# The first tile's last two probability transpositions behind the second tile's scores on TensorE

## The chip, the cores and the metric

One NeuronCore of a Trainium2 chip runs the whole program. The metric is device time in microseconds, the median of several runs. Lower is better.

## The reference

A cross-attention layer and a mixture-of-experts layer, each behind a layer norm and with a residual. The input x is 4 x 1024 x 256, the context 4 x 77 x 256, all in float32.

```python
x = x + xattn(layernorm(x), ctx, ctx, mask, Wq, bq, Wk, bk, Wv, bv, Wo, bo)   # 16 heads of 16, 77 keys
x = x + ffn(layernorm(x), gate_weight, bias, experts_gate_up, experts_down, shared_gate, shared_up, shared_down)
# xattn: softmax(q k^T / 4 where mask, else -1e9) v, then Wo and bo
# ffn:   sigmoid gate over 32 experts, the best 4 of 8 groups, then the best 6 experts, weights scaled to 2.5
#        out = sum over the 6 of w_e * (silu(x Wg_e) * (x Wu_e)) Wd_e  +  one shared expert of width 256
```

## The kernel before

The 4096 token rows are 32 tiles of 128 rows (NT = 32; t is a tile's number). The first part of the program carries each tile through attention, the second layer norm, the gate, the ranking of tokens by expert and the scattering of rows to an HBM table sorted by expert. A middle part turns counts into block addresses. The last part runs 224 blocks of 128 rows through their experts, in 112 pairs, and adds each token's six results.

Each engine has its program written out in order by `over_tiles(step)`: for n from -1 to 37, `step` lists stages, and `at_tile(tile, lag, stage)` issues the stage for tile t = n - lag if there is one. So the order of the `at_tile` lines is the order on the engine. A stage begins with waits on semaphores (`need`, `freed`, `read_out`, `wait_ge`), and what is listed behind a waiting stage waits as well.

The stages that matter here, for n = 0 and n = 1:

- TensorE: `qk` (L766 four mask products in bf16, L770 eight score products in fp32) writes the scores of tile n to `sc_ps`. It needs `qT` of its tile, and that VectorE has read the scores of the tile before (`score_sub`). `tr_x` (L740) transposes the normed x of tile n+1, `q_proj` (L750) projects it. `v_chunks` (L728), at n = 0 only, spreads the value rows over ten chunks of 128. `tr_p(f)` (L792) transposes the probabilities of a tile: 1232 columns are ten chunks (NCH = 10), `tr_p(0)` and `tr_p(1)` take four each and run at lag 1, `tr_p(2)` takes the last two and runs at lag 0, as the last stage of a step. `pv(0..2)` (L804) multiplies them with the values. `tr_o` (L815), `o_proj` (L825, L826) follow at lag 2.
- VectorE: `row_max` (L1136) and `shift` (L1144), two halves each, read the scores and write the unnormalised logits to `probs`. At n = 1 between them and the next tile's stand `late_values` (L1098: ten products that move the value chunks from PSUM to SBUF, each adding one to `vbd_ready`), then for later n `late_bias` (L1061 to L1069), `late_stats` (L1028) and the stages of older tiles (`inverse_sums` L1154, `normalise` L1159, `residual` L1166).
- ScalarE: `exps` (L591, the exponential), `ev_q` (L585, copies q with its bias to `qT`), `norm1` (L573), `ev_pT(2)` (L600), `ev_xT` (L579), `ev_pT(0)` (L600), in this order within a step. `ev_pT(1)` of a tile is first in the next step.
- GpSimd: `inverse_std` (L513) and the scattering (L493 fill, L503 indirect DMA), six rows of it for a tile.

`tr_p(2)` begins with these lines, so for the first tile it waits for the exponential and for all ten products of `late_values`. Its PSUM bank held value chunks 6 and 7.

```python
need(pe, "probs", t)
if t == 0:
    need(pe, "probs_zero", 0)
    pe.wait_ge(S_["vbd_ready"], B + NCH)
```

Of the kernel before, what the change touches and what calls it, by code (L numbers as in the profile page):

```python
# [99 lines left out]
def build(nc, x, mask, wq, wk, wv, wo, bqk, bvo, ctx_t, gate_w, gate_b, egu, edn, sgu, sdn, const_in, ids_in, out):  # L100
# [7 lines left out]
    with ExitStack() as ctx:  # L108
# [189 lines left out]
        def need(eng, name, t, per=1):  # L298
            eng.wait_ge(S_[name], (t + 1) * per)
# [10 lines left out]
        def read_out(eng, name, t, ahead):  # L310

            n = t + ahead + 1
            if not isinstance(n, int):
                eng.wait_ge(S_[name], n)
            elif n > 0:
                eng.wait_ge(S_[name], min(n, NT))
# [10 lines left out]
        def over_tiles(step):  # L327
            for n in range(-LEAD, NT + LAG):
                def tile(lag, n=n):
                    t = n - lag  # L330
                    return (t, t % UA, t // B) if 0 <= t < NT else None
                step(tile)

        def at_tile(tile, lag, stage):
            got = tile(lag)
            if got is not None:
                stage(*got)
# [9 lines left out]
        def load_table(engine, row, j, n, top):  # L347
            _, got = nc.values_load_multi_w_load_instructions(
                table[0:1, row * P + j:row * P + j + n], engines=(engine,), min_val=0, max_val=top,
                skip_runtime_bounds_check_because="the table's entries are clipped to this range where it is made")  # L350
            return got
# [338 lines left out]
        def _(pe):  # L690
# [27 lines left out]
            def v_chunks(c0, c1):  # L718
                def stage(t, m, s):
                    if t:  # L720
                        return
                    if c0 == 0:
                        need(pe, "vrows", 0, 2)
                    for c in range(c0, c1):
                        off, n0 = c * P % C, chunk_head(c) * DH
                        if c >= 6:
                            pe.wait_ge(S_["vbd_ready"], B + c // 2 * 2 - 4)
                        mm(vchunk[c].rearrange("p (b n) -> p b n", b=B), const("rep")[0:C, off:off + P],  # L728
                           vrows[0:C, :, n0:n0 + 3 * DH], start=True, stop=True).then_inc(S_["vchunk_ps"], 1)
                return stage  # L730
# [44 lines left out]
            def tr_p(f):  # L775
                def stage(t, m, s):
                    if f == 0:
                        read_out(pe, "o", t, -1)
                    if f == 1:
                        read_out(pe, "gate_exp", t, -3)  # L780
                        if 1 <= t <= 2:
                            read_out(pe, "pT1", t, -1)
                    if f == 2:
# [4 lines that stand above are left out]
                        read_out(pe, "x1", t, -2)  # L788
                        if 1 <= t <= 1:
                            read_out(pe, "pT2", t, -1)  # L790
                    for c in range(4 * f, min(4 * f + 4, NCH)):
                        last = nc.tensor.transpose(pT_ps[f][:, (c % 4) * P:(c % 4 + 1) * P],  # L792
                                                   probs[:, m % 2, c * P:(c + 1) * P], ident)
                    last.then_inc(S_[f"pT_ps{f}"], 1)
                return stage

            def pv(f):
                def stage(t, m, s):
                    need(pe, f"pT{f}", t)
                    if f == 0:  # L800
                        read_out(pe, "pT0", t, 0)
                    for c in range(4 * f, min(4 * f + 4, NCH)):
                        n0 = chunk_head(c) * PV
                        last = mm(pv_ps[:, n0:n0 + 3 * PV], pT[:, c, :], vbd[:, m, c, :, :].rearrange("p a b -> p (a b)"),  # L804
                                  start=c == 0, stop=c == NCH - 1, skip_group_check=True)
                    last.then_inc(S_["pv"], 1)
                return stage
# [71 lines left out]
            def s_up(s, h, gs=(0, 1)):  # L879
                xs = store[:, s * B * D:(s + 1) * B * D].rearrange("p (b k n) -> p k b n", b=B, k=KT)  # L880
                if s > SE:
                    pe.wait_ge(S_["shh"], 4 * (s - SE - 1) + 2 * h + 2)
                for g in gs:
                    for k in range(KT):
                        last = mm(ps8[2 * h + g].rearrange("p (b n) -> p b n", b=B),  # L885
                                  wsgu[:, k, g * SI + h * P:g * SI + (h + 1) * P],
                                  xs[:, k, :, :], start=k == 0, stop=k == KT - 1)
                if 1 in gs:
                    last.then_inc(S_["sg_ps"], 1)
# [14 lines left out]
            def count_chosen(t0, t1):  # L904
                for t in range(t0, t1):
                    last = mm(cum_ps, sel[:, t, :], stepb[:, NT - t:2 * NT + 1 - t], start=t == 0, stop=t == NT - 1)
                if t1 == NT:
                    last.then_inc(S_["cum_ps"], 1)

            def s_early(t, m, s):  # L910
                if t == NT - 3:
                    pe.wait_ge(S_["score_sub"], NT)
                if t >= NT - 3:
                    i = t - (NT - 3)
                    s_up(SE, i // 2, (i % 2,))

            def count_early(t, m, s):
                if t == NT - 1:
                    s_up(SE, 1, (1,))
                    count_chosen(0, NT - 2)  # L920

            def step(tile):
                at_tile(tile, 4, gate)
                at_tile(tile, 0, qk)
                at_tile(tile, -1, tr_x)
                at_tile(tile, -1, v_last)
                at_tile(tile, 0, v_chunks(0, 6))
                at_tile(tile, 2, tr_o)
                at_tile(tile, 1, tr_p(0))
                at_tile(tile, 1, tr_p(1))  # L930
                at_tile(tile, -1, q_proj)
                at_tile(tile, 2, o_proj)
                at_tile(tile, 3, tr_x2)
                at_tile(tile, 0, v_chunks(6, NCH))
                at_tile(tile, 4, up)
                at_tile(tile, 5, dn)
                at_tile(tile, 3, s_early)
                at_tile(tile, 4, count_early)
                at_tile(tile, 1, pv(0))
                at_tile(tile, 1, pv(1))  # L940
                at_tile(tile, 1, pv(2))
                at_tile(tile, 4, rank)
                at_tile(tile, 0, tr_p(2))
            over_tiles(step)


# [596 lines left out]
```

## Time and profile before

| | before |
|---|---|
| runs | 802.43, 800.10, 798.34 us; median 800.1 |
| the profiled execution | 801.02 us, its span 799.2 us (1.8 us lie around it) |
| TensorE busy | 734.8 us, 92% |
| VectorE / ScalarE / GpSimd busy | 522.0 (65%) / 389.7 (49%) / 535.6 us (67%) |
| mean granted TensorE clock | 0.959 |

The times of instructions are from one profiled execution and count from the start of its span. A granted clock of 1.00 is 2.4 GHz and 0.50 is 1.2 GHz. The trace counts some fp32 matmuls twice (eight score products are x16, four value products x8), transpositions once.

### The profile page before, as it was taken

How to read it: one execution, taken by the hardware profiler on the slowest of the kernel's cores; microseconds unless marked ns; L12 is line 12 of the kernel's file. 1: busy time of each engine (PE TensorE's matmuls, PEld its weight loads, DVE VectorE, ACT ScalarE, POOL GpSimd, SP SyncE). 2: the span in 40 equal slices, each digit the busy share in tenths (PEclk: the TensorE clock that was granted, in tenths of full speed). 3: DMA queues.
4: the chain of work that ended last, by engine and by line, in shares of the span. 5: the costliest groups of instructions: out<-in, count | busy, mean ns of one | idle time of the engine just before them, and what ended most of it. 6: DMA issues, size and time to landing. Idle time of an engine off the chain costs nothing.

```text
span 799.2 us, 18242 instructions
## 1 busy us (share of the span) xinstructions
PE 734.8 (92%) x5768; PEld 652.1 (82%) x5768; DVE 522.0 (65%) x1628; ACT 389.7 (49%) x832; POOL 535.6 (67%) x788
## 2 busy tenths in 40 slices
PE   6899999999999999986859999999999999999980
PEld 3789888888888888873449999998988999888970
DVE  4897777778777777665444425676775766566663
ACT  2455445444454445431026666666565666555550
POOL 0115788878787888877700007888888788987885
PEclk9899999999999999887879999999999999999995
DMA  9213443333344423432345557798888888878863
GB/s 272 94 54 100 126 133 120 120 115 131 119 133 126 134 100 126 138 120 100 107 159 170 173 167 231 243 279 248 262 261 257 252 263 250 257 239 253 259 214 108
DMA packets 97295, 140.13 MB, mean 175 GB/s; under 512 B 14944, under 2 KB 69732, under 8 KB 97201
## 3 DMA queue, kind: packets, MB, share of 16 engines
q1 hardware_dynamic: 77112, 87.50, 34.7%
q0 software_dynamic: 18432, 50.36, 20.3%
q10 hardware_dynamic: 1656, 1.10, 0.5%
q8 instruction: 48, 0.79, 0.5%
q14 instruction: 47, 0.38, 0.2%
HBM read 75.98 MB, written 62.94 MB: 174 GB/s over the span
## 4 chain that ended last, share of the span: by engine, by line
PE 36%; POOL 32%; issue 14%; DVE 8%; another core or an unknown queue 4%; DMA 2%; ACT 1%; DVEq 1%; POOLq 0%; ACTq 0%; SPq 0%
POOL rows L503 19%; PE sc_ps L994 19%; PE bank L1006 10%; POOL work L493 8%; PE sc_ps L978 4%; POOL work L541 2%; POOL rstd L513 2%; DVE firsts L1028 1%; DMA store<-in_x 1%; PE bank L898 1%; DMA work<-yrows,dest 1%; DVE work L1144 1%; DVE mx L1136 1%; PE sc_ps L885 1%
## 5 line engine op out<-in xcount | busy, mean ns | idle before, releaser
L994 PE MATMUL sc_ps<-work 128*128 128x128 f32 x1792 | 221.2, 277 | 5.9 <-DVE work L1491 2.9
L994 PEld LDWEIGHTS sc_ps<-work 128*128 128x128 f32 x1792 | 210.3, 193 | 8.7 <-issue 5.0
L541 POOL DMA_INDIRECT work<-yrows,dest x192 | 188.3, 981 | 35.6 <-POOL work L493 22.6
L503 POOL DMA_INDIRECT rows<-work,dest x192 | 187.7, 977 | 34.9 <-issue 34.8
L493 POOL MEMSET work<- 128x304 f32 (+1 forms) x360 | 136.6, 379 | 95.0 <-DMA yrows<-work 86.3
L1006 PE MATMUL bank<-wdn,work 128*128 x448 | 116.6, 383 | 5.3 <-DVE work L1446 3.3
L1446 DVE TENSOR_TENSOR work<-work,sc_ps 128x256 f32<-128x256 f32 x112 | 47.0, 419 | 113.3 <-ACT work L659 65.7
L1472 DVE SCALAR_TENSOR_TENSOR work<-work 128x256 f32<-128x256 f32 x160 | 76.9, 481 | 19.1 <-DMA work<-yrows,dest 12.7
L680 ACT ACTIVATE work<-bank 128x512 f32<-128x512 f32 x112 | 66.9, 597 | 45.5 <-PE bank L1006 25.7
L1006 PEld LDWEIGHTS bank<-wdn,work 128*128 128x128 f32 x448 | 76.5, 191 | 13.4 <-issue 7.6
L591 ACT ACTIVATE work<-work 128x1232 f32<-128x1232 f32 x32 | 39.4, 1231 | 91.1 <-DVE work L1144 81.7
L654 ACT ACTIVATE work<-sc_ps 128x512 f32<-128x512 f32 x112 | 66.7, 595 | 33.8 <-PE sc_ps L978 24.0
L659 ACT ACTIVATE work<-sc_ps 128x256 f32<-128x256 f32 x112 | 42.8, 383 | 75.2 <-PE sc_ps L994 34.1
L804 PEld LDWEIGHTS bank<-work 128*128 128x128 f32 x640 | 76.0, 192 | 1.8 <-issue 0.5
L672 ACT ACTIVATE work<-wgu 128x512 f32 x112 | 70.7, 632 | 8.8 <-issue 8.8
L804 PE MATMUL bank<-work 128*128 128x51 f32 x640 | 74.7, 272 | 0.0
L978 PE MATMUL sc_ps<-cst,work 128*128 128x128 f32 x448 | 67.7, 274 | 0.8 <-issue 0.8
L600 ACT ACTIVATE work<-bank 128x512 f32<-128x512 f32 (+1 forms) x96 | 47.3, 525 | 39.0 <-PE bank L792 38.4
L978 PEld LDWEIGHTS sc_ps<-cst,work 128*128 128x128 f32 x448 | 56.2, 142 | 12.4 <-issue 1.5
L513 POOL TENSOR_TENSOR rstd<-var,cst 128x1 f32<-128x1 f32 x32 | 18.1, 565 | 71.4 <-DVE var L1180 71.0
L1491 DVE COPY work<-wgu 128x512 f32 x112 | 57.4, 513 | 12.9 <-issue 11.3
L1136 DVE TENSOR_REDUCE mx<-sc_ps 128x8 f32<-128x616 f32 x64 | 50.8, 794 | 4.0 <-PE sc_ps L770 4.0
(173 smaller groups left out, 1108.5 us busy)
## 6 DMA issues: line engine op xcount, KB each, us to landing
work<-rows SPq DMA_DIRECT2D x224, 128.0 KB
yrows<-work SPq DMA_DIRECT2D x112, 256.0 KB
wgu<-in_egu SPq DMA_DIRECT2D x16, 512.0 KB
store<-in_x SPq DMA_DIRECT2D x8, 512.0 KB, 12.0
wdn<-in_edn SPq DMA_DIRECT2D x8, 512.0 KB
rows<-padrow SPq DMA_DIRECT2D x8, 512.0 KB
out<-work SPq DMA_DIRECT2D x32, 128.0 KB
rows<-work,dest POOLq DMA_INDIRECT x192
```

The lines of the kernel that those rows point to most:

```text
L493: pool.memset(dead, 0.0).then_inc(S_["gap"], 1)
L503: pool.indirect_dma_start(rows[:, :], bass.IndirectOffsetOnAxis(ap=dest[:, t, k:k + 1], axis=0), rowb[:, m, :], None).then_inc(scat[m], 16)
L541: pool.indirect_dma_start(yg[:, g % RG, :], None, yrows[0:2 * n * P, :], bass.IndirectOffsetOnAxis(ap=dest[:, t, k:k + 1], axis=0)).then_i ...
L654: a.activation(xeT[:, m % 2, :], ps8[m % 2], ACT.Copy).then_inc(S_["xeT"], 1)
L672: a.activation(wst[1][m % 2], wgu[:, bass.ds(named.pop(2 * i + 1) * 512, 512)], ACT.Copy).then_inc(S_["laid1"], 1)
L680: a.activation(ye[:, i % YP, :], ps8[6 + m % 2], ACT.Copy).then_inc(S_["ye"], 1)
L804: last = mm(pv_ps[:, n0:n0 + 3 * PV], pT[:, c, :], vbd[:, m, c, :, :].rearrange("p a b -> p (a b)"), start=c == 0, stop=c == NCH - 1, skip ...
L978: last = nc.tensor.transpose(ps8[m % 2][:, (2 * w + k) * P:(2 * w + k + 1) * P], xe[:, j % RX, k * P:(k + 1) * P], ident)
L994: last = mm(ps8[2 + m % 2][:, (2 * w + g) * P:(2 * w + g + 1) * P], wst[w][m % 2][:, k * 2 * I + g * I:k * 2 * I + (g + 1) * I], xeT[:, m ...
L1006: last = mm(ps8[6 + m % 2][:, w * D:(w + 1) * D], hid[:, m % 2, w * P:(w + 1) * P], wdn[:, bass.ds(e * D, D)], start=True, stop=True)
L1136: red(mx4[:, 2 * half:2 * half + 2, :], four(half), AX.X, ALU.max).then_inc(S_[f"score_max{half}"], 1)
L1472: v.scalar_tensor_tensor(outb[:, t % 3, :], yg[:, g % RG, :], slotw[:, t % 2, k:k + 1], so_far, ALU.mult, ALU.add).then_inc(S_["part"], 1)
```

## The change

The last two transpositions of tile 0's probabilities, `tr_p(2)` for t = 0, are issued in step n = 1, ahead of `tr_p(0)`, and no longer at the end of step n = 0. For every other tile `tr_p(2)` stays where it was. No wait is taken away or added, and no instruction.

```diff
+            def first_tr_p(t, m, s):
+                if t == 0:
+                    tr_p(2)(t, m, s)
+
+            def later_tr_p(t, m, s):
+                if t:
+                    tr_p(2)(t, m, s)
+
...
                 at_tile(tile, 2, tr_o)
+                at_tile(tile, 1, first_tr_p)
                 at_tile(tile, 1, tr_p(0))
                 at_tile(tile, 1, tr_p(1))
...
                 at_tile(tile, 1, pv(2))
                 at_tile(tile, 4, rank)
-                at_tile(tile, 0, tr_p(2))
+                at_tile(tile, 0, later_tr_p)
```

The only place where TensorE's order differs is the passage from step n = 0 to step n = 1. Before, its rows read (L728 value chunks, L792 the two transpositions, L766 and L770 tile 1's scores, L740 tile 2's x, L792 the other eight of tile 0, L750 tile 2's q):

```order
L750 MATMUL bank<-work 128x128 x3
L728 MATMUL bank<-wdn,cst 128x192 [waits vbd_ready] x4
L792 MATMUL bank<-cst,work 128x128 [waits vbd_ready,probs_zero,probs]
L792 MATMUL bank<-cst,work 128x128
L766 MATMUL sc_ps<-work 128x308 [waits score_sub,qT]
L766 MATMUL sc_ps<-work 128x308 x3
L770 MATMUL sc_ps<-work 128x154 x8
L740 MATMUL bank<-cst,work 128x128 [waits qT,xn]
L740 MATMUL bank<-cst,work 128x128
L792 MATMUL bank<-cst,work 128x128 x8
L750 MATMUL bank<-work 128x128 [waits xnT]
```

In the changed kernel the same place on TensorE reads:

```order
L750 MATMUL bank<-work 128x128 x3
L728 MATMUL bank<-wdn,cst 128x192 [waits vbd_ready] x4
L766 MATMUL sc_ps<-work 128x308 [waits score_sub,qT]
L766 MATMUL sc_ps<-work 128x308 x3
L770 MATMUL sc_ps<-work 128x154 x8
L740 MATMUL bank<-cst,work 128x128 [waits qT,xn]
L740 MATMUL bank<-cst,work 128x128
L792 MATMUL bank<-cst,work 128x128 [waits vbd_ready,probs_zero,probs]
L792 MATMUL bank<-cst,work 128x128 x9
L750 MATMUL bank<-work 128x128 [waits xnT]
```

The two transpositions, with their wait for the ten value products and the exponential, moved behind twelve score products and two transpositions of x. They now stand in one row with the other eight.

## Rows read from the trace of the kernel before

**Rows 1.** The page: the span, and TensorE's busy time, share and instructions.

```profile
span 799.2 us, 18242 instructions
PE 734.8 (92%) x5768; PEld 652.1 (82%) x5768; DVE 522.0 (65%) x1628; ACT 389.7 (49%) x832; POOL 535.6 (67%) x788
```

**Rows 2.** Windows, middle of the tile loop: stretch, length, busy by engine, PEclk, DMA share, GB/s.

```profile
100.00:150.00 50.00, 49.88 (x447) 44.83 (x446) 38.20 (x144) 23.45 (x55) 40.89 (x63) 1.00 0.41 130
...
200.00:250.00 50.00, 49.66 (x457) 44.48 (x456) 36.91 (x137) 24.38 (x60) 39.16 (x62) 1.00 0.39 125
```

**Rows 3.** The chain that ended last, 24 to 30 us: start, length, what.

```profile
24.64 1.58 PE bank L728 x8
...
27.02 0.66 PE bank L792 x2
27.68 1.03 PE sc_ps L766 x4
28.70 1.39 PE sc_ps L770 x16
```

**Rows 4.** Timeline, 23 to 31 us: start, length, instruction [idle before <- releaser].

```profile
23.26 0.80 DVE L1144 TENSOR_TENSOR work<-sc_ps,mx 128x616 f32<-128x616 f32 x1
23.98 2.90 DVE L1098 TENSOR_TENSOR work<-bank,cst 128x192 f32<-128x192 f32 x10
24.09 1.23 ACT L591 ACTIVATE work<-work 128x1232 f32<-128x1232 f32 x1 [2.64 <-DVE work L1144]
...
25.23 0.61 ACT L585 ACTIVATE work<-bank,bias_qk 128x128 f32<-128x128 f32 x2
...
27.02 0.66 PE L792 MATMUL bank<-cst,work 128*128 128x128 f32 x2 [0.81 <-DVE work L1098]
...
27.71 0.38 ACT L600 ACTIVATE work<-bank 128x256 f32<-128x256 f32 x1 [1.39 <-PE bank L792]
...
30.11 0.80 DVE L1136 TENSOR_REDUCE mx<-sc_ps 128x8 f32<-128x616 f32 x1 [3.17 <-PE sc_ps L770]
...
30.70 0.38 ACT L579 ACTIVATE work<-bank 128x256 f32<-128x256 f32 x1 [2.60 <-PE bank L740]
```

**Rows 5.** Windows around the changed place, columns as in group 2.

```profile
24.00:26.00 2.00, 1.36 (x8) 1.27 (x8) 2.00 (x9) 1.91 (x4) 0.00 (x0) 1.00 0.60 208
26.00:28.00 2.00, 1.19 (x7) 0.73 (x6) 0.92 (x4) 0.61 (x2) 0.00 (x0) 0.74 0.09 21
28.00:30.00 2.00, 2.00 (x20) 1.20 (x18) 0.00 (x0) 0.10 (x1) 0.00 (x0) 0.50 0.00 0
...
32.00:34.00 2.00, 2.00 (x13) 2.00 (x11) 1.90 (x5) 1.43 (x3) 0.00 (x0) 0.56 0.00 0
```

**Rows 6.** Timeline, TensorE: tile 2's scores, 36 to 38 us.

```profile
36.23 0.69 PE L766 MATMUL sc_ps<-work 77*128 77x308 bf16 x4
...
36.85 0.81 PE L770 MATMUL sc_ps<-work 32*128 32x154 f32 x16
```

**Rows 7.** Timeline, VectorE and TensorE, 36 to 39 us.

```profile
36.86 1.40 DVE L1028 BATCH_NORM_STATS2 firsts<-store 128x6 f32<-128x256 f32 x4
...
38.18 0.24 DVE L1154 RECIPROCAL rsum<-bank 128x16 f32<-128x16 f32 x1
...
38.79 0.79 DVE L1136 TENSOR_REDUCE mx<-sc_ps 128x8 f32<-128x616 f32 x1
38.93 0.20 PEld L815 LDWEIGHTS bank<-cst,work 128*128 128x128 f32 x2 [1.14 <-DVE work L1159]
```

**Rows 8.** Windows where the clock falls the second time, columns as in group 2.

```profile
50.00:55.00 5.00, 4.56 (x41) 4.04 (x44) 4.58 (x20) 3.07 (x7) 0.52 (x1) 0.93 0.14 22
55.00:60.00 5.00, 5.00 (x41) 4.27 (x33) 4.47 (x14) 1.85 (x4) 2.91 (x2) 0.73 0.24 84
```

**Rows 9.** Windows in the end of the tile loop and the middle part, as in group 2.

```profile
325.00:330.00 5.00, 3.60 (x26) 3.01 (x25) 3.10 (x14) 3.08 (x7) 4.49 (x7) 0.73 0.55 185
...
360.00:365.00 5.00, 5.00 (x14) 2.27 (x13) 1.55 (x8) 0.38 (x1) 2.31 (x4) 0.51 0.53 184
```

## The prediction

> **What bounds the kernel now.** I read the page first: TensorE is busy 92% of 799.2 us [rows 1]. The windows then say where: in the middle of the tile loop it is busy 49.88 and 49.66 of 50 us [rows 2]. There every tile waits for TensorE, and a tile loop that begins earlier ends earlier. Nothing in that stretch is touched by the change. What it touches is one place near 27 us, ahead of this full stretch, so I asked the chain of waits and the timeline for that place.
>
> The chain runs there through the value products (L728, to 24.64 + 1.58 = 26.22), a hole, the two transpositions at 27.02 and then tile 1's scores, 27.68 to 28.70 + 1.39 = 30.09 [rows 3]. The timeline names the hole: TensorE stood idle 0.81 us before L792, released by VectorE's L1098, the ten value products that end at 23.98 + 2.90 = 26.88. VectorE itself then stood 3.17 us idle until the scores came, at 30.11 [rows 4]. So at this place the engine that is waited for is TensorE, and TensorE waits for something that the scores do not need.
>
> **What the change does here.** What do the scores of tile 1 need? That VectorE has read tile 0's (L1144 ends at 23.26 + 0.80 = 24.06) and their q (L585 ends at 25.23 + 0.61 = 25.84) [rows 4]. Both are there before TensorE is through with L728 at 26.22. In the changed kernel the scores can start right behind it, at about 26.25.
>
> How long do they take? At the full clock the same twelve products took from 36.23 to 36.85 + 0.81 = 37.66, that is 1.43 us [rows 6]. In this place they took 2.41 us, since the clock was low: the granted clock is 1.00 in 24 to 26, 0.74 in 26 to 28, and 0.50 in 28 to 30 [rows 5]. From the 0.74 the fall lies near 26 + 2 x 0.48 = 26.96 us, if it is one step from 1.00 to 0.50.
>
> - No fall: scores ready at 26.25 + 1.43 = 27.68. Against 30.09 that is 2.4 us.
> - Fall at the same moment, 26.96: 0.71 us of the work is done, the other 0.72 us goes at the low clock. The low clock takes 1.39 us for L770 [rows 3] where the full one takes 0.81 [rows 6], 1.7 times as long: 1.23 us. Scores ready at 28.2, a gain of 1.9 us.
> - Low clock all through: 26.25 + 2.42 = 28.67, a gain of 1.4 us.
>
> I take 1.9, the middle one and the one that keeps the clock of the trace. Of it 0.8 us is the idle time taken away, 0.66 us the two transpositions that no longer stand ahead, and the rest is the score work that gets ahead of the fall.
>
> The two transpositions themselves cost the same as before, 0.66 us at the low clock, and are paid behind the scores. Who waits for them? On ScalarE `ev_pT(2)` (L600 at 27.71) now waits for them, and behind it in ScalarE's order stand `ev_xT` (L579, 30.70) and `ev_pT(0)`. Tile 2's x is transposed behind the scores, two transpositions like the 0.66 us at 27.02 [rows 3], so by 28.9; the two moved ones are done by 29.6, L600 (0.38 us) by 30.0 and L579 by 30.4. Before, it began at 30.70 after an idle time of 2.60 us [rows 4]. So the new order on ScalarE costs nothing; a transposition that was waiting for an idle engine still meets an idle engine. Its cover is TensorE's own eight transpositions that stand ahead of `q_proj`. Of the values L1098 is done at 26.88, well before 28.9, so the moved wait is empty. SP's and GpSimd's queues are not passed by anything.
>
> **Does the gain live until 60 us?** From 30.11 to 38.79 VectorE works almost without a gap: tile 1's maxima and shifts, the bias pieces, statistics (36.86 to 38.26), the reciprocal at 38.18, then tile 2's row maximum at 38.79. Tile 2's scores were ready at 37.66, 1.1 us before VectorE took them, and TensorE stood idle 1.14 us (weight loads) at 38.93 for VectorE's L1159 [rows 6, 7]. So VectorE sets the pace and all of it moves up by 1.9 us, provided that TensorE keeps up. TensorE's work from here to 37.66 is one piece without idle time, starts 0.77 us earlier (26.25 for 27.02) and so ends at about 36.9. VectorE would ask at 38.79 - 1.9 = 36.9. That just holds. With no fall of the clock, TensorE has far more room. After that, the next stages hang on one another by semaphores, not on an outside time: DMA is at a share of 0.00 from 28 us on [rows 5], so the loads that the start needed have landed. Once TensorE is full, it is full 1.9 us earlier.
>
> **Sum.** 801.0 - 1.9 = 799.1 us for an execution like the profiled one, and 800.1 - 1.9 = 798.2 us against the median, 0.9 us below that execution. It is 0.24%, and the three runs of before spread over 4.1 us. A measurement of this kernel can tell about 0.5%, 4 us; so the verdict should be no change.
>
> **The clock as a rule.** The clock fell after a stretch in which TensorE was busy 1.36 of 2 and 1.19 of 2 us [rows 5]. The change fills 0.8 us of that. The Trainium skill, TensorE: Matmul & The Clock Gate, Part 1, says that the gate follows how busy the array has been, and that the monitor runs freely and is not reset when a kernel starts, so that the place of a transition varies from run to run. By this rule the fall at 27 us may not come at all, and falls elsewhere may shift; the sum would then be 800.1 - 2.4 = 797.7 us by the first bullet's number. The trace agrees in that the clock fell behind idle time; one trace can't show whether the place varies.
>
> **Rivals.**
>
> 1. *The forecast*: 1.4 to 2.4 us come out at the end, 797.7 to 798.7 us. For it: the chain goes through this very place, and the engine behind it is idle 3.17 us. Against it: several steps of the tile loop lie between 38 us and the full stretch, and I followed only the first of them number by number. Chance 0.62.
> 2. *Swallowed*: the gain is used up before TensorE is full, by a later wait that I read as moving along. For it: TensorE still waits for others at 38.93 [rows 7], and the margin above (36.9 against 36.9) is nil. It would give 800.1 us, with 799.5 to 800.7 about it. Chance 0.14.
> 3. *A second fall is saved too*: in 50 to 60 us the granted clock is 0.93 and 0.73, which is 5 x 0.07 + 5 x 0.27 = 1.7 us of work lost while TensorE was busy 4.56 and 5.00 of 5 us [rows 8]. If the earlier start changes what TensorE does before it so that this fall stays away, the time is 800.1 - 2.4 - 1.7 = 796.0 us. Nothing in the change aims at it. Chance 0.10.
> 4. *Slower: a fall where TensorE is full*. A faster TensorE at 27 to 37 us waits longer for VectorE at 38.9 (1.14 us now, up to about 2 us then), and idle time is what the clock fell behind at 27. If the clock then falls for as long as from 27 to 34 us (0.52 + 1.0 + 1.0 + 0.88 = 3.4 us of work, taking 30 to 32 us as 28 to 30 [rows 5]), TensorE has about 1 us of slack a tile to pay it with and owes 2.4. If one more such fall comes in the end part, where the clock is already 0.73 and 0.51 in places with TensorE busy [rows 9], 3.4 us more are owed. The first alone gives 800.1 - 2.4 + 2.4 = 800.1 us; it decides for slower from the point where the lost work is over 3.4 us, and with 3.4 more it is 803.5 us. Chance of a time over 800.7: 0.14.
>
> **How the numbers follow.** The range takes the forecast's own width (797.7 to 798.7), the swallowed case above it, half of the way to rival 3 and the nearer part of rival 4. It has to hold the scatter of a median too, which in the runs shown is up to 2 us either way. 796.0 to 801.3 us leaves out about 0.18. Faster by over 0.5% (under 796.1 us) needs rival 3 or a lucky median: 0.08. Slower by over 0.5% (over 804.1 us) needs rival 4 with a second fall: 0.03. The same: 0.89.
>
> **What would show it.** In the profile after: L766 right behind L728 near 26.3 us, without the 0.81 us idle time; the row maximum at 27.7 to 28.7 us for 30.11; L792 as one group of ten behind L740; ScalarE's L579 no later than 30.7; the row maximum of tile 2 near 36.9 us for 38.79; GpSimd's first scatter about 1.9 us earlier. I am wrong if the scores start late because q or L1144 isn't there, if VectorE's stages at 38 us don't move by as much as those at 30, or if the first scatter moves and the end doesn't, which would be the clock in the end part.

## The result, and the profile after

| | before | changed |
|---|---|---|
| median of 22 runs each, side by side | 798.46 us (789.64 to 807.26) | 793.80 us (786.10 to 803.46) |
| ratio changed / before | | 0.9952, 95% interval 0.9930 to 0.9975 |
| the profiled execution | 801.02 us, span 799.2 | 793.72 us, span 791.9 |
| mean granted clock of it | 0.959 | 0.968 |

The ratio is worked out from the fast runs alone, those within 1.5% of the fastest of their kernel, so it is not the quotient of the two medians, 0.9942. The changed kernel is faster by 0.48%, just inside the 0.5% that I had called no change, and beyond its interval. I had said 798.2 us, from 796.0 to 801.3; 793.8 lies outside. Of the 4.4 us by which I missed, 1.6 us is the base: the kernel before has a median of 798.46 us in 22 runs, not 800.1 as in three. By the ratio, the gain is 798.46 x 0.0048 = 3.8 us (2.0 to 5.6 by its interval), where I had 1.9.

The chain of waits of the changed kernel, 24 to 29 us (start, length, what), answers to [rows 3]:

```profile
24.65 1.57 PE bank L728 x8
26.22 0.52 PE sc_ps L766 x4
26.74 0.78 PE sc_ps L770 x16
27.55 0.81 DVE mx L1145
```

The hole is gone: the scores follow the value products at once. The lines of VectorE are nine further down than before, so L1145 is the row maximum. The timeline of the changed kernel for the same place answers to [rows 4, 7]; its columns are start, length, instruction, and in brackets the idle time before it and what ended it:

```profile
23.98 2.90 DVE L1107 TENSOR_TENSOR work<-bank,cst 128x192 f32<-128x192 f32 x10
...
26.06 0.69 PE L766 MATMUL sc_ps<-work 77*128 77x308 bf16 x4
...
26.67 0.81 PE L770 MATMUL sc_ps<-work 32*128 32x154 f32 x16
...
27.55 0.80 DVE L1145 TENSOR_REDUCE mx<-sc_ps 128x8 f32<-128x616 f32 x1 [0.59 <-PE sc_ps L770]
...
27.68 1.26 PE L792 MATMUL bank<-cst,work 128*128 128x128 f32 x10
28.10 0.39 ACT L600 ACTIVATE work<-bank 128x256 f32<-128x256 f32 x1 [1.77 <-PE bank L792]
...
28.38 0.38 ACT L579 ACTIVATE work<-bank 128x256 f32<-128x256 f32 x1
...
36.22 0.79 DVE L1145 TENSOR_REDUCE mx<-sc_ps 128x8 f32<-128x616 f32 x1
36.35 0.20 PEld L815 LDWEIGHTS bank<-cst,work 128*128 128x128 f32 x2 [2.24 <-DVE work L1168]
```

The scores ran at the full clock, 0.69 and 0.81 us, where they had taken 1.03 and 1.39. The row maximum comes at 27.55 for 30.11, tile 2's at 36.22 for 38.79: 2.56 and 2.57 us. ScalarE's L579 comes 2.3 us earlier, so the moved pair holds up nobody there. TensorE now waits 2.24 us for VectorE at 36.35, for 1.14 before.

What becomes of the 2.57 us? GpSimd's L513 runs once a tile, so its starts are good milestones for the tile loop. For tiles 0, 1 and 2 the changed kernel has

```profile
44.76 0.55 POOL L513 TENSOR_TENSOR rstd<-var,cst 128x1 f32<-128x1 f32 x1 [21.44 <-DVE var L1189]
52.91 0.55 POOL L513 TENSOR_TENSOR rstd<-var,cst 128x1 f32<-128x1 f32 x1 [7.60 <-DVE var L1189]
...
62.63 0.54 POOL L513 TENSOR_TENSOR rstd<-var,cst 128x1 f32<-128x1 f32 x1 [6.29 <-DVE var L1189]
```

and the kernel before

```profile
46.33 0.55 POOL L513 TENSOR_TENSOR rstd<-var,cst 128x1 f32<-128x1 f32 x1 [23.03 <-DVE var L1180]
54.48 0.55 POOL L513 TENSOR_TENSOR rstd<-var,cst 128x1 f32<-128x1 f32 x1 [7.60 <-DVE var L1180]
...
65.76 0.54 POOL L513 TENSOR_TENSOR rstd<-var,cst 128x1 f32<-128x1 f32 x1 [7.85 <-DVE var L1180]
```

So 1.57 us is left at tile 0, and 3.13 us at tile 2. Both steps come where the clock differs. The windows of the changed kernel (stretch, length, busy time of TensorE, its weight loads, VectorE, ScalarE and GpSimd, then the granted clock, the DMA share and GB/s):

```profile
24.00:34.00 10.00, 9.27 (x91) 7.83 (x92) 9.04 (x25) 6.37 (x13) 0.00 (x0) 1.00 0.10 33
34.00:44.00 10.00, 8.00 (x50) 6.93 (x51) 8.78 (x23) 4.27 (x9) 0.00 (x0) 0.83 0.04 5
```

```profile
50.00:55.00 5.00, 4.57 (x49) 3.98 (x49) 4.50 (x21) 2.95 (x10) 2.09 (x2) 1.00 0.35 105
55.00:60.00 5.00, 5.00 (x42) 4.50 (x40) 3.96 (x14) 2.51 (x6) 1.34 (x1) 1.00 0.12 16
```

The fall at 27 us is gone, one at 37 us is new (0.83 in 34 to 44), and the fall at 54 us, 0.93 and 0.73 in [rows 8], is gone too. From tile 2 on the gain stays between 2.8 and 4.1 us to tile 29. The last 3.4 of the 7.3 us between the two spans come behind it, in the middle part and the expert part, where neither kernel's order was changed and the clock falls in both.

### The profile page after: what moved, and what is told of

Same layout as the page of the kernel before. It is cut to its first block, busy times and chain, and to the rows that moved or that the text cites. A ratio compares the mean times of both kernels' runs of the same rounds, so it can differ in the third digit from the quotient of the medians.

```text
span 791.9 us, 18242 instructions
## 1 busy us (share of the span) xinstructions
PE 727.0 (92%) x5768; PEld 647.6 (82%) x5768; DVE 521.1 (66%) x1628; ACT 389.0 (49%) x832; POOL 535.1 (68%) x788
## 4 chain that ended last, share of the span: by engine, by line
PE 37%; POOL 31%; issue 16%; DVE 6%; another core or an unknown queue 4%; DMA 3%; ACT 1%; SPq 1%; POOLq 0%; DVEq 0%; ACTq 0%
PE sc_ps L1003 20%; POOL rows L503 20%; PE bank L1015 10%; POOL work L493 7%; PE sc_ps L987 5%; POOL rstd L513 2%; DMA store<-in_x 2%; POOL work L541 2%; PE bank L898 1%; DMA yrows<-work 1%; PE bank L804 1%; ACT work L672 1%; DVE work L1153 1%; DVE mx L1145 0%
## 5 line engine op out<-in xcount | busy, mean ns | idle before, releaser
L804 PEld LDWEIGHTS bank<-work 128*128 128x128 f32 x640 | 75.9, 192 | 1.8 <-issue 0.5
L804 PE MATMUL bank<-work 128*128 128x51 f32 x640 | 74.7, 272 | 0.0
L513 POOL TENSOR_TENSOR rstd<-var,cst 128x1 f32<-128x1 f32 x32 | 18.1, 565 | 66.2 <-DVE var L1189 65.7
L1153 DVE TENSOR_TENSOR work<-sc_ps,mx 128x616 f32<-128x616 f32 x64 | 51.2, 799 | 1.2
```

Source lines behind the costliest of these rows:

```text
L1153: last = tt(probs[:, m % 2, 0:HC].rearrange("p (r h c) -> p r h c", r=4, h=4)[:, 2 * half:2 * half + 2], four(half), mx4[:, 2 * half:2 * h ...
```

## The experiments

Twelve runs, in three groups: c0, a1, e1, e2; then c1, e3, e4, e5; then c2, a2, e3b, e4b. The kernel before ran beside each group; its medians there were 780.9, 818.3 and 779.7 us. The first and the third group ran on one chip, the second on another, so chips differ by far more than the change is worth, and ratios are taken inside a group. In the profiles I count from the start of the last value products (L728 x8, 24.64 us in the first profile). In all profiles but a2 and e4 it lies between 23.57 and 24.65 us; in these two it comes at 30.04 and 29.33 us. In the table "max 1" is tile 1's row maximum, "rstd 0" to "rstd 20" are GpSimd's L513 of these tiles; "wait" is TensorE's idle time ahead of the first `tr_o`, where it waits for VectorE to normalise tile 0 (L1159 in the kernel before).

| profile | clock falls at, up to 130 us | max 1 | wait | rstd 0 | rstd 2 | rstd 20 |
|---|---|---|---|---|---|---|
| before, first | 27, 54 | 5.47 | 0.91 | 21.69 | 41.12 | 233.37 |
| c0, before | 27, 54 | 5.47 | 0.92 | 21.69 | 41.12 | 231.56 |
| c1, before (the slower chip) | 38 | 4.16 | 2.01 | 21.38 | 39.25 | 238.71 |
| c2, before | 27, 54 | 5.37 | 0.76 | 21.58 | 41.06 | 231.50 |
| changed, first | 37 | 2.90 | 2.00 | 20.11 | 37.98 | 229.36 |
| a1, changed | 35 | 2.89 | 2.01 | 21.31 | 39.17 | 229.62 |
| a2, changed | 15, 42 | 3.88 | 2.00 | 20.96 | 38.82 | 229.26 |
| e1, wait kept | 27 | 4.94 | 0.36 | 21.15 | 39.01 | 229.45 |
| e2, hole filled | 36 | 4.12 | 2.01 | 21.13 | 38.98 | 229.42 |
| e3, stats late (the slower chip) | 104 | 2.90 | 0.70 | 17.16 | 34.42 | 235.99 |
| e3b, stats late | 123 | 2.89 | 0.70 | 17.15 | 34.41 | 227.74 |
| e4, second hole (the slower chip) | 15, 59 | 5.20 | none | 21.76 | 41.25 | 242.57 |
| e4b, second hole | 51 | 2.90 | 0.47 | 19.10 | 38.55 | 229.00 |
| e5, late hole (the slower chip) | 38 | 4.16 | 2.01 | 21.34 | 39.21 | 238.33 |

### Both kernels again: c0, a1, c1, a2, c2

No edit in any of them.

> The kernel before once more, unchanged, beside itself. What it tells: where the clock falls in another execution, and how far two medians of the same kernel lie apart. Theory A (the fall near 27 us belongs to the order of the work: TensorE idles 0.8 us there): the granted clock falls again between 24 and 30 us, tile 1's row maximum comes at 28.7 to 30.1 us, and the ratio is 1.000 within 0.4%. Theory B (the fall is chance, it came in the one profile that was read): no fall before 34 us, row maximum at about 28.9 us.

> The changed kernel once more. Theory A: no fall before 35 us, row maximum of tile 1 at 27.5 us as in its first profile, ratio 0.995. Theory B: the fall near 27 us can come here as well, the row maximum then at 28.2 us or later, and the ratio is 0.997 to 0.998, the 1.9 us of the forecast.

> The kernel before a third time, for the place of its falls alone. Theory A: falls near 27 and near 54 us again, tile 1's row maximum 5.5 us behind the value products, rstd of tile 1 to tile 2 in 11.3 us. Theory B: one of the falls is missing.

> The changed kernel a third time. Theory A (of the change's gain 1.1 to 1.3 us is order and shows at equal clock, the rest is clock time not lost, which varies from execution to execution): tile 1's row maximum 2.9 us behind the value products, a fall of the clock at 35 to 38 us, ratio 0.995 to 0.998; in a fit of the time by the clock time lost the kernel's own term is -1.1 us within its error. Theory B (the whole 3.8 us of the first comparison belong to the change, in every execution): ratio 0.995, own term -3 us or more.

> The kernel before a fourth time, for its falls before 60 us: near 27 and 54 us as in two executions, or at 38 us alone as in the third. The order part of the gain should be the difference of tile 1's row maximum between executions with no fall there, 4.16 - 2.90 = 1.26 us behind the value products; with a fall at 27 us it is 5.47 - 2.90 = 2.57 us.

Measured: before against itself 1.0014 (0.9979 to 1.0049); the changed kernel 0.9977 (0.9942 to 1.0011) and 0.9976 (0.9942 to 1.0009). Weighted by the widths of their intervals, the three comparisons of the changed kernel make 0.9963 +- 0.0016, that is 2.9 us +- 1.3.

Is the fall at 27 us the order's or chance's? Both have a part. Up to 52 us e5 has the order of before. So that order has five executions, and the fall came in three (the first profile, c0, c2), not in c1 and e5. It came in e1, which keeps the wait. It came in none of the five executions with the changed order that reached the place at the full clock (the first profile, a1, e3, e3b, e4b), nor in e2, where the wait is filled. That is four of six with the idle time and none of six without; a2 and e4, low from 15 us on, say nothing of it. Why the fall stayed away in c1 and e5 is not known. Timeline of c1, the kernel before with the full clock all through this place:

```profile
24.10 1.57 PE L728 MATMUL bank<-wdn,cst 77*128 77x192 f32 x8 [0.77 <-DVE work L1098]
...
26.48 0.41 PE L792 MATMUL bank<-cst,work 128*128 128x128 f32 x2 [0.81 <-DVE work L1098]
26.77 0.68 PE L766 MATMUL sc_ps<-work 77*128 77x308 bf16 x4
27.39 0.81 PE L770 MATMUL sc_ps<-work 32*128 32x154 f32 x16
...
28.26 0.80 DVE L1136 TENSOR_REDUCE mx<-sc_ps 128x8 f32<-128x616 f32 x1 [1.85 <-PE sc_ps L770]
```

The hole of 0.81 us stands there as in the others, and the row maximum comes 4.16 us behind the value products instead of 5.47. So the order alone is worth 4.16 - 2.90 = 1.26 us, and the fall at 27 adds 1.31 us in the executions that have it. e5 has the 4.16 as well, and the four other full-clock executions of the changed order 2.89 or 2.90. a2, the changed kernel, had a low clock from 15 to 32 us, which begins ahead of the change:

```profile
30.04 2.55 PE L728 MATMUL bank<-wdn,cst 77*128 77x192 f32 x8
...
33.92 0.80 DVE L1145 TENSOR_REDUCE mx<-sc_ps 128x8 f32<-128x616 f32 x1 [0.59 <-PE sc_ps L770]
...
42.73 0.69 PE L815 MATMUL bank<-cst,work 128*128 128x128 f32 x2 [2.00 <-DVE work L1168]
```

Its last value products begin 5.8 us later than in a1 (24.27), more than the change brings. Counted from there it is like the other two: 38.82 at tile 2 and 229.26 at tile 20.

The column "wait" shows a second pattern. In the six executions where TensorE waited 2.00 or 2.01 us for tile 0's output, the clock fell in that wait or up to 1.3 us behind it: three of the changed kernel (37, 35, 42 us), but also c1, e2 and e5 (38, 36, 38 us), which have the order of before. In the seven with a wait of 0.36 to 0.92 us it did not fall there. All six had tile 1's scores at the full clock, and the other executions at the full clock there (e3, e3b, e4b) have an edit that shortens this wait. So the longer wait comes with a full clock at 27 us, in either order, and the change alone does not open it. c1, with the order of before:

```profile
37.08 0.44 PE L815 MATMUL bank<-cst,work 128*128 128x128 f32 x2 [2.01 <-DVE work L1159]
```

How does a gain travel? On the faster chip a tile takes 10.58 us in the full stretch. From tile 2 to tile 20 it is 190.44 or 190.45 us in seven executions (c0, c2, a1, a2, e1, e2, e4b). a1 is 1.95 us ahead of c0 at tile 2 and 231.56 - 229.62 = 1.94 us ahead at tile 20, and 1.7 us at tile 31. In the span it is 0.3 us ahead, 777.1 for 777.4: the rest went behind the tile loop, where executions that were level differ by 2 to 3 us. The slower chip's tiles are less even, and so are those of the first comparison, where 3.13 us at tile 2 became 4.0 at tile 20.

But c1, the unchanged order with no fall at 27 us, is at 39.25 at tile 2 (e5 at 39.21; both on the slower chip), level with a1's 39.17. The 1.26 us of order that a1 had at tile 1 went in its longer low clock behind the 2.01 us wait. So how far the changed kernel is ahead depends on which falls the execution of before has: 1.9 to 3.1 us at tile 2 against one with falls at 27 and 54 us (41.06 to 41.12 for 37.98, 39.17 and 38.82), 0.1 to 1.3 us against c1.

The runs of the first and the third group come with their mean granted clock, so the time can be set against the clock time that each run lost, (1 - clock) x time, by a straight line with a term of its own for each kernel. In the first group there are 83 runs of five programs: 0.77 us for each us of clock lost, and 1.4 us of scatter left of about 4. The changed kernel's own term is -1.1 +- 0.5 us (one standard error) and in the third group -1.0 +- 0.5 (e3b -1.3, e4b -1.4); before against itself +0.2 +- 0.5. On the slower chip the line leaves 3.4 us of scatter and tells nothing. The mean clock lost is 31.1 us for before and 29.2 for a1 in the first group, 30.2 and 29.1 in the third. 1.9 x 0.77 = 1.5 us and 1.1 x 0.79 = 0.9 us would be the clock's part; but the two differences have standard errors of 1.7 and 1.4 us, so this part is not shown by the runs. The own term is the 1.26 us of the profiles within its error, as theory A said; B, -3 us in every execution, does not hold.

### e1: the wait kept

```diff
                 freed(pe, "score_sub", t, 1)
+                if t == 1:
+                    need(pe, "probs", 0)
+                    pe.wait_ge(S_["vbd_ready"], B + NCH)
```

> The changed order, but tile 1's scores still wait for the ten value products and the exponential, so the 0.8 us idle time stays and only the two transpositions are out of the way. Theory A: the clock falls near 27 us as before, row maximum of tile 1 at 27.0 + 2.4 = 29.4 us, that is 0.7 us of gain; ratio 0.999. Theory B (the gain at this place is order alone): 28.5 us at the full clock or 29.4 us at the low one, as chance has it.

Measured: 0.9982 (0.9939 to 1.0024), own term -0.8 +- 0.5 us. In its timeline TensorE waits and the low clock is back:

```profile
24.18 1.57 PE L728 MATMUL bank<-wdn,cst 77*128 77x192 f32 x8 [0.77 <-DVE work L1110]
26.55 1.16 PE L769 MATMUL sc_ps<-work 77*128 77x308 bf16 x4 [0.81 <-DVE work L1110]
27.64 1.41 PE L773 MATMUL sc_ps<-work 32*128 32x154 f32 x16
```

Row maximum 4.94 us behind the value products; 29.4 - 24.6 = 4.8 was expected from the fall and the two transpositions out of the way. A gain of only 0.53 us there. Yet at tile 2 it is 2.11 us ahead of the kernel before, as far as a1, and stays there, since the fall at 54 us did not come. So that much at tile 2 can be had with the wait kept. It is one execution, and theory B's low-clock case, 29.4 us, is the same number: e1 alone does not tell A from B.

### e2: the hole filled

```diff
                            vrows[0:C, :, n0:n0 + 3 * DH], start=True, stop=True).then_inc(S_["vchunk_ps"], 1)
+                    if c1 == NCH:
+                        for _ in range(6 if c == NCH - 1 else 0):
+                            nc.tensor.transpose(sc_ps[:, 3, 320:320 + P], ident, ident)
```

> The order of before, with six transpositions of the identity matrix put into the idle time, into unused columns of the scores' PSUM; their results are read by nobody. The dependencies stay as before. Theory A: TensorE no longer idles at 26.2 to 27.0 us, the clock does not fall there, and tile 1's row maximum comes at 27.0 + 0.4 + 1.4 = 28.9 us instead of 30.1, so that half of the change's gain comes with nothing moved; ratio 0.997 to 0.998. Theory B (the clock is chance and the fill does nothing): row maximum at 30.1 us where the clock falls, ratio 1.000 or a little above.

Measured: 0.9944 (0.9907 to 0.9980); I had expected 0.997 to 0.998. The medians, 778.29 us beside 780.93, give 0.9966. Timeline, with the filling as L732:

```profile
23.57 1.57 PE L728 MATMUL bank<-wdn,cst 77*128 77x192 f32 x8 [0.77 <-DVE work L1101]
...
24.98 0.82 PE L732 MATMUL sc_ps<-cst 128*128 128x128 f32 x6
...
25.95 0.41 PE L795 MATMUL bank<-cst,work 128*128 128x128 f32 x2
...
27.69 0.80 DVE L1139 TENSOR_REDUCE mx<-sc_ps 128x8 f32<-128x616 f32 x1 [1.81 <-PE sc_ps L773]
```

Row maximum 4.12 us behind, 4.26 expected: with nothing moved and TensorE kept at work, the scores come 1.35 us earlier. One profile does not show that the filling did it, since c1 and e5 have 4.16 with the wait left empty. The runs support it: the 12 of e2 lie between 775.9 and 779.1 us, narrower than any other set of nine runs or more, and lost 26.9 us of clock on the mean for 31.1, a difference of 4.2 us with a standard error of 1.0. Its own term is -0.7 +- 0.5 us, though in this place the filled kernel does the same work in the same order; I take it as a measure of how far such a term can be trusted: the -1.1 and -1.0 of the changed kernel are not much further from nothing than this.

### e4: the second hole filled

TensorE's new wait at 36 us, in the changed kernel. The wait of `tr_o` for ScalarE's copy of `pT2` stands ahead of the filling.

```diff
             def tr_o(t, m, s):
-                need(pe, "o", t)
                 read_out(pe, "pT2", t, 1)
+                if t == 0:
+                    for _ in range(14):
+                        nc.tensor.transpose(bank[0][:, 320:320 + P], ident, ident)
+                need(pe, "o", t)
```

> The changed kernel with 14 transpositions of the identity matrix in the 2.0 us in which TensorE waits for tile 0's normalised output at 34.4 to 36.4 us; nobody reads them. Theory A (the earlier start opens a longer wait at 36 us, behind which the clock falls and takes back 1.0 us in one profile and 2.2 us in the other): no fall between 30 and 45 us, the first GpSimd rstd comes 2.6 us before that of the kernel before, counted from the value products at 24.6 us, that is 19.1 us behind them for 20.1 and 21.3; ratio 0.993 to 0.996. Theory B (the fall at 36 us is chance): it comes or stays away as it likes, no earlier rstd than 20.1.

> The changed kernel with 14 idle transpositions in the 2 us wait at 34.4 to 36.4 us, a second time, since the first profile had a long low clock from 15 us on, ahead of its edit. Theory A (the fall at 35 to 38 us hangs on this idle time): with a full clock at the start, no fall at 35 to 38 us and the first rstd 19.1 us behind the value products for 20.1 and 21.3 in the changed kernel. Theory B (it does not): a fall there as in the changed kernel, 20.1 us or more.

The first profile had the low clock from 15 to 39 us, ahead of the edit, and the four runs give 1.0143 (1.0078 to 1.0208). Why they are slower is open: the one profile has its low clock ahead of the filling, and the twelve runs of e4b on the faster chip are not slower. The second: 0.9953 (0.9919 to 0.9988). Its windows, and its timeline around the filling (L813):

```profile
24.00:34.00 10.00, 9.71 (x95) 8.28 (x96) 8.89 (x24) 6.09 (x14) 0.00 (x0) 1.00 0.09 28
34.00:44.00 10.00, 9.06 (x82) 7.73 (x80) 9.13 (x25) 4.42 (x9) 0.55 (x1) 1.00 0.08 17
...
50.00:60.00 10.00, 9.91 (x78) 8.80 (x78) 7.53 (x26) 5.16 (x12) 3.43 (x2) 0.83 0.31 77
```

```profile
33.74 1.69 PE L813 MATMUL bank<-cst 128*128 128x128 f32 x14
35.91 0.44 PE L818 MATMUL bank<-cst,work 128*128 128x128 f32 x2 [0.47 <-DVE work L1171]
```

No fall at 35 to 38 us, and the first rstd 19.10 us behind the value products, the 19.1 expected, for 20.11 and 21.31. All 2.6 us of the early gain are there at tile 0. Then the clock fell at 51 us, and tile 2 was reached at 38.55. So the fall at 36 us is what eats the early gain in the changed kernel. This is one execution, but it fits the column "wait": all six executions with the 2 us wait fell there, and the filled one did not. When one fall is removed another may come.

### e3: the statistics later

```diff
-                if t == 1:
-                    x_stats(4)
-                if t == 2:
-                    x_stats(5)
-                    x_stats(6)
-                if t == 3:
-                    x_stats(7)
+                if 5 <= t <= 8:
+                    x_stats(t - 1)
+                if t == 8:
                     x_variance(2)
-                if t == 9:
+                if t == 11:
                     x_shift(2)
...
-                if t == 1:
+                if t == 6:
                     inverse_part(2)
```

> The changed kernel, with VectorE's statistics of tiles 16 to 31 (28 us of starting tiles before, 5.6 us of VectorE work between 34 and 52 us) taken in steps 6 to 9 instead of 2 to 4, where TensorE sets the pace. Theory A (the stretch from 27 to 60 us is VectorE's, and a microsecond gained there lives to the end of the tile loop): TensorE no longer waits 2 us at 36 us, tile 2's GpSimd rstd comes 3 us or more before the changed kernel's, ratio to before 0.990 to 0.993. Theory B (gains ahead of the full stretch are swallowed): the rstd of tile 10 comes at the changed kernel's time, ratio 0.995 to 0.998.

> The changed kernel with the statistics of tiles 16 to 31 taken later, a second time, beside the changed kernel itself. Theory A (what is gained before TensorE is full lives on): the rstd of tile 2 about 34.4 us behind the value products for 38 to 39, and that of tile 20 at least 3 us before the changed kernel's in the same call; ratio 0.990 to 0.994. Theory B (the later statistics take back what they gave, VectorE holding up TensorE in steps 6 to 9): tile 20 no earlier than the changed kernel's, ratio 0.995 to 0.999.

Measured: 0.9991 (0.9936 to 1.0045) and 0.9980 (0.9937 to 1.0023). The early part did what it should: no wait at 36 us, tile 2 at 34.4 us behind the value products, 6.6 us ahead of the kernel before in the same group for e3b (c2) and 4.8 us for e3 (c1). Then it is lost again. GpSimd's rows of e3b, 100 to 136 us:

```profile
100.92 0.57 POOL L513 TENSOR_TENSOR rstd<-var,cst 128x1 f32<-128x1 f32 x1 [1.15 <-DVE var L1185]
101.47 2.91 POOL L477 TENSOR_TENSOR rstd<-firsts,cst 128x16 f32<-128x16 f32 x1
113.34 0.58 POOL L513 TENSOR_TENSOR rstd<-var,cst 128x1 f32<-128x1 f32 x1
123.25 0.57 POOL L513 TENSOR_TENSOR rstd<-var,cst 128x1 f32<-128x1 f32 x1 [0.40 <-DVE var L1185]
135.38 0.57 POOL L513 TENSOR_TENSOR rstd<-var,cst 128x1 f32<-128x1 f32 x1 [2.59 <-DVE var L1185]
```

GpSimd's inverse root L477 takes 2.91 us; at 54 us it stood in idle time, at 101 us it stands among the scatters, where GpSimd had 1.15 us of idle time in that tile, and the next tile is 12.42 us behind instead of 10.58. The clock then fell at 123 us (12.13 us for that tile). At tile 20 it is 3.8 us ahead of c2, but only 1.5 us ahead of a2 of the same group and 1.9 us ahead of a1, where theory A had at least 3 us ahead of the changed kernel: that expectation failed. Of the 4.8 us by which it led a1 at tile 2, 2.9 are gone: 1.55 in the tile with the low clock (12.13 for 10.58), and about 1.3 in the tiles around L477. Theory B, no lead at all, failed too. In the time, nothing of it can be told from the changed kernel.

### e5: the late hole filled

```diff
+                    if t == 2 and f == 2:
+                        for _ in range(3):
+                            last = nc.tensor.transpose(bank[3][:, 320:320 + P], ident, ident)
                     last.then_inc(S_["pv"], 1)
```

> The kernel before, with three transpositions of the identity matrix behind tile 2's value products, in the 0.43 us in which TensorE waits at 52.7 us; nobody reads them, everything ahead stays as before. Theory A (the fall at 54 us in both profiles of before hangs on how busy TensorE was just ahead, and its absence is worth 1.6 us): falls near 27 us again, none at 54 us, rstd of tile 1 to tile 2 in 9.7 us instead of 11.3, as in all four shifted kernels. Theory B (the fall at 54 hangs on the time at which it is reached, not on the idle time): the fall stays, 11.3 us.

Measured: 1.0066 (1.0023 to 1.0109). In the profile neither the fall at 27 nor that at 54 came, and 9.71 us from tile 1 to tile 2. That looks like theory A, but c1, the kernel before in the same group, had neither fall either. The run does not tell the theories apart. The signal `pv` now comes behind the three transpositions, but tile 2 is not later for it (39.21 for c1's 39.25). Why its time was 0.7% over that of before I can't say: its profile shows low stretches of the clock at 250, 663 and 738 us which c1 has not, and which the edit is not near.

## Why the prediction was right or wrong

- *The scores can start at 26.25 us.* Right: 26.22 in the chain. All they needed was there.
- *How long they take*: I gave three cases, 2.4, 1.9 and 1.4 us, and took the fall at the same moment. In the changed kernel it was the first case, 2.56 us, in both profiles with a full clock up to there. The paragraph on the clock as a rule had named this case, but the sum did not go by it. The step that failed is "the one that keeps the clock of the trace": 1.9 us was taken, 2.56 us measured. The fall went with TensorE's idle time: it came in four of six executions that have the 0.81 us wait and in none of six that have it not. The order itself is 1.26 us, below every number I gave, since I had counted some lost clock in each.
- *ScalarE and the moved wait cost nothing.* Right, L579 came 2.3 us earlier.
- *VectorE sets the pace to tile 2.* Right, 2.57 us of 2.56 arrive at 36.22.
- *The gain lives until 60 us, since there is no outside time.* Half right. Nothing outside held it, but 1.0 us (first profile) and 2.2 us (a1) of it went in a new low stretch at 35 to 38 us. That was rival 4's place, and its longer wait: 2.00 us where I had "up to about 2 us". e4b, with the wait filled, has no such fall. I had priced the fall at up to 3.4 us and had put only the outcome over 800.7 us at 0.14, with no chance for the fall itself; it came in all three executions of the changed kernel (a2's at 42 us, behind the same 2.00 us wait), and none of the three comparisons is slower. What I missed is that it goes with the full clock at 27 us and not with the order, since c1, e2 and e5 have it too.
- *Falls elsewhere were put at nothing in the sum.* Wrong. This is the larger mis-sized term: the fall at 54 us, 1.6 us (11.28 against 9.72 us from tile 1 to tile 2), came in every execution of before that had the one at 27, and in none of the five profiles of the changed kernel, e1 and e2. That the change keeps it away is not shown: c1 and e5 went without it too, and e4b, with the changed order, had one at 51 us. That was rival 3, chance 0.10. Together in the first profile 2.57 - 1.00 + 1.56 = 3.13 us, in a1 2.58 - 2.20 + 1.56 = 1.94 us, measured 1.95 at tile 2.
- *A gain ahead of the full stretch reaches the end of the tile loop.* Right to the hundredth from tile 2 to tile 20 on the faster chip (1.95 and 1.94), and 1.7 us at tile 31. Behind the tile loop it can't be told from the 2 to 3 us by which level executions differ there.
- *The base.* The median of three runs was 1.6 us high, and the range of 5.3 us had no room for it beside a gain of twice the size. Over all three comparisons the gain is 2.9 +- 1.3 us, which holds the 1.9 that I forecast; the first alone, 3.8, does not quite. 793.8 us was out of the range by the base and the clock together. That 2.9 +- 1.3 holds the forecast 1.9 is in part luck: the place gave 2.56, and two falls that the sum had at nothing went one each way.

What stays open is why the fall at 54 us goes away. In c1 it stayed away with the order of before, where the work stood 0.3 us earlier; in e4b one came at 51 us. Idle time is not its only condition, and the one experiment on it, e5, did not tell. Open too is the expert part, where spans differ by 2 to 3 us between executions that were level before it.

## What to carry to other kernels

Look for a wait that stands in an engine's order ahead of work that doesn't need it, and price it to the next full stretch of the bounding engine: if nothing outside sets a time, it travels through that stretch whole (190.44 or 190.45 us for 18 tiles in seven executions here). Where the wait is TensorE's, reckon in the clock on both sides: the low clock behind the idle time may go, and a new wait further on may bring one, each worth as much as the move itself (1.31 us, and 1.0 and 2.2 us, here, beside 1.26). To size an effect below 0.5%, compare milestones inside the trace, counted from a common point, and set each run's time against the clock it lost; medians of a few runs can't.

## What the runs showed of the hardware that I had not expected

- A wait of 2.00 or 2.01 us on TensorE was followed by the low clock, at once or within 1.3 us, in six of six executions, one of 0.36 to 0.92 us at the same place in none of seven; one of 0.81 us at 27 us in four of six.
- With six idle transpositions (0.82 us) in a 0.81 us wait the same scores came 1.35 us earlier in the one profile, and the twelve runs lay at 775.9 to 779.1 us, with before at 775.4 to 789.6.
- The run-to-run scatter of this kernel goes mostly with TensorE's clock: 0.77 us of time for each us of lost clock, 1.4 us of scatter left of about 4.
- One program had the clock low from 15 to 32 us in one execution (a2) and full in two others, and its last value products began at 30.04 us for 24.27 and 24.65, before anything of the change was reached. The Trainium skill, TensorE: Matmul & The Clock Gate, Part 1, says that the monitor runs freely and that transitions vary from run to run; here the traces agree, with places that differ between executions of one program (before: 27 and 54 us in three, 38 us alone in c1).
- Chips differ: 780.9 and 779.7 us in two groups on one chip and 818.3 us on another for the same kernel, with 10.58 us a tile on the first and about 11.1 on the second, while the mean duration of TensorE's instructions was the same (L804 at 272 ns in c0 and c1).
